# Waits between the first gathers of a graph kernel's Pool queue

## What is computed

```python
h = jnp.maximum(_layernorm(x), 0.0)               # 3125 x 160
s, v = h[:, :64] @ W_nl0, project(h[:, 64:], W_nl1)
rhat = edge_attr / norm(edge_attr)
w = relu(edge_feature @ W_fc1) @ W_fc2            # 224 numbers per edge
xs, xv = s[dst], v[dst]                           # a row of 160 gathered per edge
tp = products(w, xs, xv, rhat)                    # five kinds of products
agg = segment_sum(tp, src) / 32                   # a sum per node: scatter-add
out = x + gated(agg @ W_out + skip(h))
```

## Time and profile before

| | |
|---|---|
| median of three runs | 1414.35 us (1413.16 to 1416.03) |
| the profiled execution, its own time | 1413.66 us |
| its span | 1411.9 us |
| POOL busy | 1072.1 us, 76% |
| PE busy | 965.4 us, 68% |
| DVE busy | 913.6 us, 65% |
| ACT busy | 430.2 us, 30% |
| instructions | 26567 |

### The profile page before, as it was taken

How to read it: one execution, slowest core, us unless ns; L and a number is a source line. 1 busy time by engine, 2 the same in 40 slices (tenths; PEclk the granted TensorE clock), 3 DMA queues, 4 the chain that set the end, 5 groups by cost and what they waited for, 6 DMA issues and landing times.

```text
span 1411.9 us, 26567 instructions
## 1 busy us (share of the span) xinstructions
PE 965.4 (68%) x5852; PEld 814.8 (58%) x5852; DVE 913.6 (65%) x3779; ACT 430.2 (30%) x844; POOL 1072.1 (76%) x826
## 2 busy tenths in 40 slices
PE   7125886777776767578657877685767677678935
PEld 5124775666665646466646766564656557567832
DVE  7603886767566667667675767565675667678625
ACT  5002433333323333333323233232333233234302
POOL 1773888888888888888888888888888888887870
PEclk9556988887778878878878788787798877898977
DMA  9522454545455454545454545545545455546556
GB/s 356 137 66 49 81 102 81 101 79 102 82 83 96 81 103 80 99 82 102 81 100 78 104 80 91 90 80 102 80 87 94 81 104 90 91 79 107 54 71 249
DMA packets 123502, 139.60 MB, mean 99 GB/s; under 512 B 34177, under 2 KB 98369, under 8 KB 123394
## 3 DMA queue, kind: packets, MB, share of 16 engines
q0 software_dynamic: 78720, 73.65, 36.6%
q1 hardware_dynamic: 44674, 64.99, 14.7%
HBM read 86.30 MB, written 52.26 MB: 98 GB/s over the span
## 4 chain that ended last, share of the span: by engine, by line
SPq 41%; issue 29%; DMA 13%; POOL 10%; PE 3%; DVE 2%; ACT 1%; another core or an unknown queue 0%; POOLq 0%; DVEq 0%; ACTq 0%
SPq L346 32%; DMA sums<-to_add,add_idx 6%; SPq L341 6%; POOL sums L423 6%; DMA sums<-spare,add_idx 4%; POOL turn_space L405 2%; POOL spare L405 1%; DMA ef<-edge_t 1%; SPq L299 1%; POOL rows L405 1%; SPq L306 1%; SPq L305 1%; DMA sums<-spare 1%; DMA turn_space<-sums 0%; PE t_ps L606 0%
## 5 line engine op out<-in xcount | busy, mean ns | idle before, releaser
L541 PE MATMUL o_ps<-w,pT 128*128 128x96 f32 (+1 forms) x2496 | 367.1, 302 | 80.4 <-ACT pT L666 43.0
L541 PEld LDWEIGHTS o_ps<-w,pT 128*128 128x128 f32 (+1 forms) x2496 | 348.6, 216 | 115.7 <-issue 92.4
L423 POOL DMA_INDIRECT sums<-to_add,add_idx x208 | 333.1, 1601 | 87.0 <-issue 74.6
L423 POOL DMA_INDIRECT sums<-spare,add_idx x204 | 326.2, 1599 | 62.4 <-issue 56.7
L675 ACT ACTIVATE msg<-o_ps 128x448 f32<-128x448 f32 x208 | 113.2, 544 | 501.7 <-remote 272.6
L525 PE MATMUL t_ps<-w,products_space 128*128 128x128 f32 (+1 forms) x1248 | 219.5, 304 | 58.0 <-DVE products_space L874 41.5
L556 PE MATMUL d_ps<-msg,same 128*128 128x192 f32 x824 | 209.4, 386 | 33.9 <-ACT to_add L687 13.2
L666 ACT ACTIVATE pT<-t_ps 128x512 f32<-128x512 f32 (+1 forms) x312 | 186.0, 596 | 144.5 <-remote 65.6
L405 POOL DMA_INDIRECT turn_space<-node_table,to_idx x186 | 185.6, 998 | 56.7 <-issue 50.6
L556 PEld LDWEIGHTS d_ps<-msg,same 128*128 128x128 f32 x824 | 167.4, 233 | 79.0 <-issue 74.3
L525 PEld LDWEIGHTS t_ps<-w,products_space 128*128 128x128 f32 (+1 forms) x1248 | 168.8, 159 | 75.0 <-DVE products_space L874 40.1
(11 more groups left out here) (125 smaller groups left out, 991.5 us busy)
## 6 DMA issues: line engine op xcount, KB each, us to landing
from_row<-nodes_row SPq DMA_DIRECT2D x52, 512.0 KB
ef<-edge_t SPq DMA_DIRECT2D x52, 256.0 KB
turn_space<-node_table SPq DMA_DIRECT2D x768, 0.6 KB
spare<-node_table SPq DMA_DIRECT2D x768, 0.6 KB
sums<-zeros SPq DMA_DIRECT2D x6, 672.0 KB, 9.5
spare<-sums SPq DMA_DIRECT2D x9, 384.0 KB, 8.6
sums<-to_add,add_idx POOLq DMA_INDIRECT x208
sums<-spare,add_idx POOLq DMA_INDIRECT x204
```

What stands on the lines that cost most here:

```text
L423: pool.indirect_dma_start(sums[t], bass.IndirectOffsetOnAxis(ap=add_idx[:, 2 * v + h, j:j + 1], axis=0), to_add[2 * v + h][:, j, :], None, ...
L541: ins = nc.tensor.matmul(o_ps[m][:, base + oc:base + oc + n], pT[c][u % 2][:, cols], w[0:ROWS[c], wc:wc + n], start=(q == 0 and c == 0), s ...
```

## The change

```diff
 AHEAD = 7
+PACED = range(6, 2 * AHEAD)
+BEHIND = 6
 SKEW = 3
...
                     elif b == UNROLL // 2 and h == 0:
                         pool.wait_ge(skip_out, 16 * 3)
+                    if 2 * b + h in PACED:
+                        pool.wait_ge(out_copied, 2 * (2 * b + h - BEHIND) + 2)
                     for j in range(J):
                         if j == BY_ROW_J and 2 * b + h in BY_ROW:
                             continue
```

## The result

The changed kernel takes 1424.3 us, the median of seven runs (1420.85 to 1427.2); the kernel before, in seven runs beside it, 1414.35 (1411.61 to 1416.96). In two later sets of runs the ratio was 1.0085 (1.0070 to 1.0101) and 1.0048 (1.0029 to 1.0067).

What follows compares the result with a forecast made beforehand. Pool was taken to bound the kernel from its first scatter on; that scatter, at 149.0 + 10.1 + 0.4 = 159.5 us, comes 26 us later than 133.47, so 1413.66 + 26 = 1439.7, written 1440, range 1426 to 1457.

Steps and rivals of the forecast that it cites:

- What bounds the kernel: Pool from first scatter to last: some 1241 us of work, 37.5 us behind; the end moves with the first scatter.
- Theory A: Experiments' expectation for Pool: the first scatter follows the last copy waited for plus gathers; the end moves one for one.
- The gathers hold the engines: In the fill, Pool's back-to-back gathers hold up the other engines' sequencers; group 0's messages are copied only near 122 us.
- The first rival: In the fill, SP's row loads or first passes through code cause the hold: first scatter 65 us late, 1479 us; 7%.
- Release and group 0: After group 5's gathers: hold ends between 70.7 and 76.0 us, group 0's second copy starts at 83 us.
- figure for the low clock in GHz: For PE's remaining group 0 work, 8.7 us: a granted clock of 0.50 was called 1.2 GHz.
- Groups 1 to 7: Message copies in the fill: 9.36 us per group, 65.5 us for seven, kept from the kernel before.
- lower bound of 8.1: DVE's own work per group: 57 us for seven, some 2 less; first scatter at 147, 13.5 late.
- Behind the first scatter: Pool's part after the fill: nothing removed, again 1241 us; the other engines' lead buys nothing beyond some 4 us.
- The second rival: In the fill, each paced group's gathers bring their own hold: nearer 11.05 us per group, 1446 to 1457 us; 20%.
- The range: For the whole kernel's time: 1426 to 1457 us, taking in the worked-out forecast and the bursts, leaving out 17%.
- The third: Behind the first scatter, Pool itself runs faster, from 37 ns per instruction: stretch under 1236 us, 1411 or lower; 5%.

Runs made afterwards that it cites:

- e7: Changed kernel with only the first of its eight waits (group 6 for group 0's messages), where the hold is; ratio 1.0005 to the kernel before.
- e3: Kernel before plus one wait, group 14's gathers for group 7's messages, in the set without the hold; 1407.4 us against 1397.5 with a single early wait.
- e13: The changed kernel unedited, in another set with the hold; 1421.29 us, 5.0 above the kernel before of its set.
- e12: Kernel before with SP's first row loads put off until group 0's first messages are copied, where the hold is; 1414.67 us against 1413.85.
- e8: Changed kernel with only the first wait, group 0's scatters right after group 6's gathers; 1407.04 us against the kernel before's 1413.88, ratio 0.9957.
- e11: e8 waiting for group 0's first message copy, with groups 6 and 7 gathered ahead of the scatters; 1405.21 us against the kernel before's 1413.85, ratio 0.9936.
- e14: The kernel of e11 again in another set; 1403.79 us against the kernel before's 1416.26, ratio 0.9922.
- e10: Changed kernel with each wait for the first of the two message copies instead of the second; first scatter at 143.43 us, no total time given.
- e1: Changed kernel with only the first of its eight waits, in the set without the hold; 1397.49 us, ratio 1.0001 to the kernel before.
- e4: Kernel before with SP's first row loads put off until group 0's messages are copied, in the set without the hold; 1400.42 us.

## Why the prediction was wrong in size

**What bounds the kernel: right.** The end follows the first scatter. Pool's stretch from the first scatter to the end of the last was 1240.9 us before and 1238.7 after; in the other runs with the order of the change or of before it was 1237 to 1245, save e7's. What lay behind it was 36.4 to 37.8 us (35.0 to 37.9 in the set without the hold). Theory A's one for one held in e3 to 1.4 us, in the profiled pair to 2, and in e13's set not better than to 6.

**The gathers hold the engines: right**, shown by the changed kernel (the hold ended with the gathers, while SP's row loads went on), by e7 (the hold came back with 36 more gathers in a row) and by e12 (no row loads, full hold). The first rival is out. What the rows show held are steps on SP's queue and the starts of instructions; by which path no run shows.

**Release and group 0: a little late.** The prediction let the hold last 2.2 to 7.5 us behind the last gather; it was 0.5. Against that, PE had not finished step 1: transposes and the copy of the hidden layer took until 71.90, some 3.4 us and not 1.5. The copy started at 79.97, not 83: 3.0 us of the error. The prediction's figure for the low clock in GHz is in no trace: they show it as 0.50 of full speed, at which the 8.7 us were read.

**Groups 1 to 7: the step that failed.** It took the 9.36 us per group of the kernel before, "because it is of the same steps of the same code". It was 8.08: 65.5 - 56.6 = 8.9 us. Together with the 3.0 that is the whole error of the first scatter, 159.5 foretold and 147.7 measured. The 8.08 equals the prediction's lower bound of 8.1 partly by luck. DVE's work in the seven periods was 49.4 us, 7.05 per group, and not the 55 of that bound, which took out some 2 us for one group's comparisons where two groups' are missing.

The same code ran in another state: in the kernel before PE began these steps at the low clock, straight out of the hold that the change was to remove, and its first period was 4.4 us longer (11.95 against 7.51). The low clock accounts for it: PE's six groups of matmuls from 124.33 us took 9.71 us, and the same six one step later, at the high clock, 5.31. The other 4.5 us lie in the later six periods, with Pool's gathers and scatters beside them. The second low clock lies there too: from 177.68 to 184.93 us five groups of matmuls took 3.3 us more than at the high clock. The changed kernel had a shorter such stretch of its own (granted 0.50 from 98 to 100 us), with 1.6 us more, so the clock is worth at most 1.7 of the 4.5. How the rest divides stays open.

e3's engines made a group in 7.36 us beside Pool's gathers, which held nobody there; in the changed kernel a group took 8.08. By the same number the changed kernel was still 5.0 us above that over seven groups, 3.9 of it in the first three; the two runs are from different sets, so this is a comparison and not a test.

**Behind the first scatter: 2.2 us given back** in the profiled pair, so that 12.3 us are left of 14.25. In the medians it was 10.0, 13.4 and 5.0 us in three sets; the stretch varies by some microseconds between runs of either kernel.

**The second rival** (a hold for each burst, 11.05 us per group) did not come at its size: the rate fell from 9.36. Its mechanism is there, though. In six of the seven periods ACT's first message copy came 1.7 to 2.7 us behind the end of PE's matmuls for it, and in e3 0.04 us behind. In the last four periods DVE had other work meanwhile and waited at most 0.7 us for the copy; in groups 1 and 2 it waited 1.9 and 3.3. **The third**, a faster Pool, did not come: scatters took 1.62 us in the mean, and 1.60 before. That the change is slower was right, and so was its reason, that the fill can't win while seven groups at 8 us each stand ahead of the first scatter. The range ended 1.7 us too high not because of the fill: its bottom put the first scatter at 147, and it came at 147.72. The bottom then counted that delay one for one (1413.66 + 13.5 = 1427.2), with 1 us to spare. The profiled execution gave back 2 us behind the first scatter, and the median lies 1.65 below that execution.

## What to carry to other kernels

Where a queue is the bound from a certain point on, a wait put ahead of that point costs what it delays that point by, whatever it does for the other engines; relief for them pays only if their result is what the queue waits for next. So pause once, for the first result, and consume it at once, rather than pace the whole fill: the pause alone won nothing (e7), with early scatters it won 7 to 12 us (e8, e11, e14). And a rate read where the engines came out of a stall is not the rate for a run without the stall (here 9.36 and 8.08 us per group): read the granted clock and the idle times of each period first, and count the busiest engine's work per group as a likely value, not as the far bound.

## What the runs showed of the hardware

While Pool issued 60 indirect gathers back to back and SP no row loads (e12), DVE did 1.08 us of work, ACT 1.79 and PE 8.86 in the 36 us from 64 to 100, and ACT stood for 39.3 us in front of one copy. In the changed kernel the hold ended 0.5 us behind the last of 24 gathers, in the kernel before 7.5 us behind the last of 60.

A short hold cost more than its own time in e10, some 2 us of it and 3 of a lower clock of PE: PE was busy 0.64 of 2.61 us, and the next 4.5 us ran at a granted clock of 0.50, against 1.00 ahead of 117.55.

Whether the gathers hold anybody is not in the kernel alone. In one set of four the same 56 gathers in a row held nobody (e3: 32 row loads in 14.8 us, no wait of the kind called "remote" in its list of waits), and the kernel before took 1397.5 us instead of 1414 to 1416, and the first scatters of e1 and e4 came at 116 us. What differs between the chips, or between their states, was not found.
